# A graph network kernel: the third weight part of every second batch is multiplied on GpSimd

## What is computed

```python
def _spmm(src, dst, w, x, n):
    return jax.ops.segment_sum(w[:, None] * x[src], dst, num_segments=n)
...
msg = h[src] * norm[:, None]
out = jax.ops.segment_sum(msg, dst, num_segments=n_nodes)
```

## Time and profile before

| | us |
|---|---|
| median of the runs | 1826.44 |
| span of the profiled execution | 1822.0 |
| PE busy in it | 1704.3 (94%) |
| VectorE busy | 942.9 (52%) |
| ScalarE busy | 569.8 (31%) |
| GpSimd busy | 186.2 (10%) |
| mean granted TensorE clock | 0.989 of full |

### The profile page before, as it was taken

The page is one execution under the profiler, slowest core; times in us unless marked ns, Lnnn a source line. Parts: engine busy times, 40 slices in busy tenths (PEclk is TensorE's granted clock), DMA queues, the critical chain, the costliest instruction groups (busy, mean ns, idle before and its releaser), DMA issues.

```text
span 1822.0 us, 30852 instructions
## 1 busy us (share of the span) xinstructions
PE 1704.3 (94%) x10162; PEld 1363.7 (75%) x10163; DVE 942.9 (52%) x1593; ACT 569.8 (31%) x854; POOL 186.2 (10%) x260
## 2 busy tenths in 40 slices
PE   6999999888879999999999999999999999998995
PEld 4898988888766777777777777767677777787784
DVE  7999999998862300111144443552312243245436
ACT  2135677888880100000011111343400000004442
POOL 4000000000000100000000000000000000153683
PEclk9999999999999999999999999999999999999998
DMA  4203344544569445454443435900054434434375
GB/s 98 1 34 124 146 175 192 206 201 200 228 239 356 132 139 154 134 161 149 138 127 110 127 124 149 232 1 0 15 187 167 141 110 120 151 117 132 106 241 183
DMA packets 136919, 261.73 MB, mean 144 GB/s; under 512 B 22236, under 2 KB 74735, under 8 KB 136606
## 3 DMA queue, kind: packets, MB, share of 16 engines
q1 hardware_dynamic: 116824, 237.02, 40.2%
q0 software_dynamic: 5808, 14.70, 2.2%
q10 hardware_dynamic: 14230, 9.29, 1.7%
HBM read 161.13 MB, written 108.09 MB: 148 GB/s over the span
## 4 chain that ended last, share of the span: by engine, by line
issue 55%; PE 27%; ACT 6%; DVE 4%; ACTq 3%; DMA 2%; POOL 1%; DVEq 1%; SPq 0%; POOLq 0%
PE ps L2112 12%; PE ps L2113 4%; PE ps L2143 3%; ACT wide L870 3%; ACTq L914 2%; PE ps L2363 2%; ACT ps L818 2%; PE ps L2347 2%; DVE act_c L1373 1%; PE ps L2355 1%; PE ps L2339 1%; PE ps L2160 0%; ACTq L859 0%; DMA count_matrix<-wide 0%; PE ps L2015 0%
## 5 line engine op out<-in xcount | busy, mean ns | idle before, releaser
L2143 PE MATMUL ps<-wide 128*128 128x320 f32 (+1 forms) x2000 | 533.2, 427 | 0.0
L2143 PEld LDWEIGHTS ps<-wide 128*128 128x128 f32 x2000 | 378.4, 190 | 141.3 <-issue 0.4
L2112 PE MATMUL ps<-early,act_c 128*128 128x200 bf16 x2400 | 295.7, 252 | 43.4 <-issue 18.7
L2143 PE MATMUL ps<-wide,act_a 128*128 128x320 f32 (+1 forms) x1000 | 264.4, 426 | 2.3 <-DMA wide<-weight_matrix 2.2
L2112 PEld LDWEIGHTS ps<-early,act_c 128*128 128x128 bf16 x2400 | 220.5, 97 | 58.1 <-issue 57.3
L2143 PEld LDWEIGHTS ps<-wide,act_a 128*128 128x128 f32 x1000 | 189.8, 190 | 75.4 <-DMA wide<-weight_matrix 2.4
L870 ACT COPY wide<-ps 128x832 f32<-128x832 f32 x200 | 169.8, 849 | 121.8 <-PE ps L2113 120.6
L818 ACT ACTIVATE ps<-wide 128x832 f32 (+1 forms) x200 | 173.4, 868 | 42.0 <-ACT wide L870 33.7
L1373 DVE TENSOR_TENSOR act_c<-act_a,pair_tab 128x3072 bf16<-128x3072 bf16 x98 | 169.1, 1750 | 14.6 <-PE ps L2113 14.6
L1501 DVE TENSOR_TENSOR wide<-ps,rows 128x1280 f32<-128x1280 f32 x10 | 14.9, 1491 | 283.5 <-PE ps L2160 283.5
L2112 PE MATMUL ps<-act_a,act_c 128*128 128x200 bf16 x1152 | 140.3, 251 | 11.0 <-ACT ps L818 4.2
(11 more groups left out here) (261 smaller groups left out, 1808.5 us busy)
## 6 DMA issues: line engine op xcount, KB each, us to landing
wide<-weight_matrix SPq DMA_DIRECT2D x90, 800.0 KB, 4.5
wide<-count_matrix SPq DMA_DIRECT2D x45, 800.0 KB, 4.6
weight_matrix<-wide SPq DMA_DIRECT2D x60, 480.0 KB, 2.5
count_matrix<-wide SPq DMA_DIRECT2D x60, 480.0 KB, 2.6
weight_matrix<-wide SPq DMA_DIRECT2D x20, 560.0 KB, 2.7
count_matrix<-wide SPq DMA_DIRECT2D x20, 560.0 KB, 2.7
wide<-weight_matrix SPq DMA_DIRECT2D x20, 400.0 KB, 3.7
routed_tokens<-in_x_dram SPq DMA_DIRECT2D x2, 3072.0 KB, 30.4
```

The lines of the kernel that those rows point to most:

```text
L2112: nc.tensor.matmul(weights, hot_parts[:, slot % PART_SLOTS, part, two, :, k], hot_key[mask_slot][:, mask_two, 0:WCOLS, k], start=False, st ...
L2143: i = nc.tensor.matmul(ps[:, 2 * sub + h, 0:n], features[:, q * QUADS + t, h * P:(h + 1) * P], moving, start=q == 0 and t == 0, stop=q == ...
```

## The change

On every second batch (`slot % 2 == 1`) VectorE's product covers only the first two weight parts. The third is made by a new loop on GpSimd, one `tensor_tensor` per line of 128 x 1024 bf16 elements with both inputs in SBUF. It waits for `hot_lane` of its line and for the same point of `pair_done` as VectorE, and raises `thirds_made`, on which TensorE waits before the second batch of each line. On TensorE and ScalarE the register that a wait compares with passes through a bitwise "and" with 2047 first, which leaves its value as it is. Two semaphores of later weight loads are made one. What is added in the branch `disordered > 0` doesn't run with these inputs.

```diff
@@ TensorE, ScalarE: register waits
-                    act.wait_ge(pair_done, end)
+                    act.wait_ge(pair_done, act.scalar_reg_alu(ALU.bitwise_and, end, COUNTED))
...
-                            pe.wait_ge(acc_free, nc.s_assert_within(free, 1, WINDOWS // GROUP, skip_runtime_bounds_check_because="a group's number plus one"))
+                            pe.wait_ge(acc_free, pe.scalar_reg_alu(ALU.bitwise_and, free, COUNTED))
                             if half == 0:
                                 pe.wait_ge(batch_ready, step * UNROLL + batch + 1)
+                            if half == 0 and weighed_by_pool(batch):
+                                pe.wait_ge(thirds_made, step * MASK_SLOTS + batch // MASK_BATCHES + 1)
@@ GpSimd, after stage_end(pool, 1)
+            def third_parts(step, turns):
+                for half in range(turns):
+                    both_batches = step * MASK_SLOTS + half
+                    pool.wait_ge(lane_made, both_batches + 1)
+                    for b in range(MASK_BATCHES):
+                        slot = half * MASK_BATCHES + b
+                        if weighed_by_pool(slot):
+                            pool.wait_ge(pair_done, (both_batches + 2) * MASK_PAIRS + b * BATCH)
+                            third = slice(2, 3)
+                            pool.tensor_tensor(hot_parts[:, slot % PART_SLOTS, third], of_lanes(half, b, third), of_weights(step, slot, third), ALU.mult).then_inc(thirds_made, 1)
+
+            with pool.Fori(0, TURNS) as step:
+                third_parts(step, MASK_SLOTS)
+            third_parts(TURNS, TURNS_LEFT)
@@ VectorE
-                            pair_weights = pair_weight[:, ds(step * UNROLL + slot, 1), :, :].rearrange("p g j (a k) -> p (g j) a k", k=2)
-                            weighed = [P, 3, TWOS, P, 2]
+                            parts = slice(0, 2 if weighed_by_pool(slot) else 3)
                             dve.wait_ge(pair_done, (both_batches + 2) * MASK_PAIRS + b * BATCH)
-                            dve.tensor_tensor(hot_parts[:, slot % PART_SLOTS], hot_lane[half][:, b * TWOS:(b + 1) * TWOS].unsqueeze(1).broadcast_to(weighed),
-                                              pair_weights.unsqueeze(3).broadcast_to(weighed), ALU.mult).then_inc(batch_ready, 1)
+                            dve.tensor_tensor(hot_parts[:, slot % PART_SLOTS, parts], of_lanes(half, b, parts), of_weights(step, slot, parts), ALU.mult).then_inc(batch_ready, 1)
...
             compute_end(dve, 1)
+            dve.wait_ge(thirds_made, BATCHES // MASK_BATCHES)
@@ TensorE, in front of the last layer
-            pe.wait_ge(moe_w1_loaded, 16 * MOES)
-            pe.wait_ge(moe_w2_loaded, 16 * MOES)
+            pe.wait_ge(moe_weights_loaded, 16 * 2 * MOES)
```

More of the change, by code:

```diff
@@ L75 @@
 UNROLL = MASK_SLOTS * MASK_BATCHES
+COUNTED = 2047
 BATCHES = -(-STEPS_P // MASK_PAIRS) * MASK_BATCHES
@@ L467, in build_program @@
         lane_made = sem("lane_made")
+        thirds_made = sem("thirds_made")
         batch_ready = sem("batch_ready")
@@ L504, in build_program @@
         gcn_in = sem("gcn_in")
-        moe_w1_loaded = sem("moe_w1_loaded")
-        moe_w2_loaded = sem("moe_w2_loaded")
+        moe_weights_loaded = sem("moe_weights_loaded")
         biases_loaded = sem("biases_loaded")
@@ L574, in over_banks, with weighed_by_pool, of_weights, of_lanes @@
             return ps_flat[:, bank * 512:bank * 512 + PPAD]
+        def weighed_by_pool(slot):
+            return slot % MASK_BATCHES == 1
+        def of_weights(step, slot, parts):
+            weights = pair_weight[:, ds(step * UNROLL + slot, 1), parts, :].rearrange("p g j (a k) -> p (g j) a k", k=2)
+            return weights.unsqueeze(3).broadcast_to([P, parts.stop - parts.start, TWOS, P, 2])
+        def of_lanes(half, b, parts):
+            return hot_lane[half][:, b * TWOS:(b + 1) * TWOS].unsqueeze(1).broadcast_to([P, parts.stop - parts.start, TWOS, P, 2])
         def block_t_ps(bank, b):
@@ L722, in _ @@
                         here_e = slice(e * D, (e + 1) * D)
-                        sp.dma_start(moe_w1[:, :, here_e], a["L1_ffn_w1"][e].rearrange("(k p) n -> p k n", p=P)).then_inc(moe_w1_loaded, 16)
-                        sp.dma_start(moe_w2[:, :, here_e], a["L1_ffn_w2"][e].rearrange("(k p) n -> p k n", p=P)).then_inc(moe_w2_loaded, 16)
+                        sp.dma_start(moe_w1[:, :, here_e], a["L1_ffn_w1"][e].rearrange("(k p) n -> p k n", p=P)).then_inc(moe_weights_loaded, 16)
+                        sp.dma_start(moe_w2[:, :, here_e], a["L1_ffn_w2"][e].rearrange("(k p) n -> p k n", p=P)).then_inc(moe_weights_loaded, 16)
                     sp.dma_start(moe_b1, a["L1_ffn_b1"].rearrange("e n -> (e n)").partition_broadcast(P)).then_inc(biases_loaded, 16)
@@ L2092, in _ @@
                             pair(g, par)
+                pe.drain()
+                pe.sem_inc(pair_done, PPAD)
+                pe.sem_inc(lane_made, BATCHES // MASK_BATCHES)
             with pe.If(disordered < 1):
```

## The result

The changed kernel takes 1894.95 us, the median of four runs (1890.23 to 1901.01), against 1826.2 for the kernel before (four runs; the three of the first table had 1826.44). The ratio is 1.0385, with a 95% interval of 1.0364 to 1.0406. The prediction was 1914.5, within 1868 to 1990: slower, and by 20 us less than forecast. The profiled execution is the fastest of the four and has a span of 1888.5 us, 66.5 more than before.

The account below looks back on a forecast made before the run. VectorE was taken to bound the build's first half, with TensorE close behind. 74 lines x 7.83 = 579.4 us against 489.3 gave +90, corrected to +88: span 1910, plus 4.4 to the median, 1914.5, range 1868 to 1990.

Parts of the forecast that it names:

- What bounds the kernel: Matrix build: VectorE sets the pace in the first half at 6.34 us a line; ScalarE, TensorE and VectorE alternate later.
- TensorE's own pace: 5.90: Matrix build: TensorE needs 5.90 us a line, 16 pairs at 5.8 plus 0.1, the second limit 0.44 under VectorE.
- rival A: Matrix build: no exclusion, TensorE's 5.90 decides, 40 lines gain 0.44 us each, 18 us, to 1808; chance 0.09.
- Relief of 0.54 us: VectorE's line in the build: 1024 of 3072 elements fewer in one product takes 6.34 us to 5.80.
- Exclusion: Matrix build: GpSimd's product and VectorE's two-input stream exclude each other, so a line takes 5.80 + 2.03 = 7.83 us.
- Its size: Matrix build: a GpSimd product of 2.22 us, less handover, keeps VectorE away for 2.03 us per line.
- The two corrections: Late part and end of build: VectorE's 14.4 us of waits shrink to 3; ScalarE's 12.3 us tail to about 7, -5.
- Who wins doesn't matter: Matrix build: whichever engine gets the port first, each line holds VectorE's stream and GpSimd's 2 us.
- the second case: Matrix build: VectorE keeps GpSimd out, TensorE stops, VectorE runs out of free `hot_parts` buffers and pauses, giving GpSimd 2 us.
- The "ands" at 0: TensorE's sequencer in the build: four register operations per line, 296 in all, hidden while TensorE waits for VectorE; 0 us.
- The bound of 9.5 us: TensorE's sequencer in the build: cost of 296 "and" operations at 32 ns if all were exposed.
- The falling clock: Matrix build: exclusion plus TensorE idle 1.93 us a line lowers its clock; half the lines low gives about 2020; chance 0.07.

Follow-up runs that it names:

- relief with GpSimd silent: Changed kernel without GpSimd's product, "ands" kept; on every second batch nobody makes the third part and TensorE takes the second twice: 1841.66 us, ratio 1.0078.
- the product apart: Kernel with the "ands" alone, VectorE making all three parts, plus one GpSimd product per line between buffers of its own that nothing waits for: 1933.22 us, ratio 1.0576.
- the copy: Kernel with the "ands" alone, VectorE making all three parts, plus a GpSimd copy of 1024 bf16 elements per line between its own buffers: 1865.27 us.

## The prediction against the result

**What bounds the kernel: half right.** VectorE was busy without a gap, but it wasn't the only limit. "TensorE's own pace: 5.90" failed. It came from one stretch of 16 matmuls and one gap of 0.23 us, among the smallest; the others run to 1.4. Over whole stretches TensorE needs 6.42 to 6.57 us with the "ands" and 6.34 to 6.42 with half of them. It changed neither sign nor sum, since VectorE's 7.51 lies above, but it made rival A's 1808 wrong, at least with the "ands" in: relief with GpSimd silent gave 1841.7.

**Relief of 0.54 us: right.** The product of 2048 elements takes 1.21 us, and a line without the exclusion would be 7.51 - 1.70 = 5.81.

**Exclusion: right in kind.** VectorE's two-input stream and GpSimd's reads take turns, as rows 5 and 6 had it for other forms. The handshake is cleared by the product apart, which nobody waits for. The section "Who interferes with whom" in the Trainium skill's "SBUF — State Buffer" has the case as the runs show it, with the memset as its other half: a GpSimd instruction that only writes doesn't contend with a two-input VectorE instruction, and 951 ns of memset per line cost nothing. The prediction also took from this section that the lock is held for a whole instruction, and the section gives it to whoever issues first. There the measurement decides: VectorE lost 1.70 us where GpSimd's instruction is never shorter than 1.95, and a GpSimd instruction issued at 101.10 us stood behind every VectorE instruction of the next 96 us.

**Its size: the term that was mis-sized.** I took 2.03 us per line; it is 1.70. The row of 1.95 us for 896 elements gives GpSimd's duration, I scaled it to 2.22, and I took the hold on the port to be nearly all of it. Both steps were too high. VectorE loses the time of the reads alone, 2048 x 0.83 ns = 1.70. The median duration of 2.36 contains a wait for its turn of some 0.4 us, and the shortest, 1.95, is still 0.25 over the hold. 74 x 0.33 is 24 us of the sum's error. The two corrections came to -4.3 where I had -5, and to nothing where I had left 3; the 4.1 us after the build weren't in the sum. They and a median 6.5 us above the profiled span, where I had 4.4, took back 6 of the 27 us by which those terms were too high. So that the forecast is only 20 us off is in part luck.

**Who wins doesn't matter: right for the sum, and for a reason I had only half.** In the changed kernel GpSimd's product nearly always got in at the next boundary. Where nothing waited for it, it once stood 98 us, and the lines still came to 8.04 us on the mean. My reason for the second case, that TensorE stops and so forces VectorE to pause, wasn't put to the test: in the changed kernel no product took over 3.5 us.

**The "ands" at 0: right, as the run with twice as many shows.** The bound of 9.5 us for the exposed case was too low: a register operation shown with 32 ns costs TensorE 64 when its sequencer sets the pace.

**The falling clock: didn't happen.** TensorE's matmuls are idle 1.6 us in every line and its weight loads 1.8, less than the 2.08 us in front of the one fall of the earlier trace rows, and from 101 us on the granted clock stays at 1.00. With the product apart, where single waits reached 5.8 us, it did fall, and the stage was no longer for it.

## What to carry to other kernels

Work moved from a full VectorE to GpSimd isn't parallel when VectorE's instructions have two SBUF inputs: count what GpSimd reads, all inputs together, at the 0.83 ns per element and partition measured here for bf16, and add it to VectorE's time. Here 0.54 us went and 1.70 came. Before relieving an engine that is busy 100%, take away its work with nobody doing it and see what the kernel gains; here, with the "ands" in, it was nothing. And read the second engine's pace over a whole stretch, not over its best line.

## What was new about the hardware

- GpSimd's hold on the port is in proportion to the elements it reads: 1.70 us for 2 x 1024, 0.84 for 2 x 512, 0.84 for 1 x 1024, and none for 1024 written. It is 0.2 to 0.25 us shorter than the shortest durations of the same instructions.
- A GpSimd instruction can stand 98 us (136 and 116 in the runs with half the product and with the copy) in front of a VectorE stream without gaps, each of whose instructions is shorter than 2 us. In the changed kernel the longest of 74 took 3.5 us. All the long waits began in the first product of a line, but others that began there were short. What decides this wasn't found.
- The wait for the port is part of the waiting instruction's duration on VectorE, so its busy share rises from 52% to 54% with less work to do.
- A register operation shown with 32 ns in TensorE's sequencer costs 64 to 70 ns where the sequencer sets the pace, and nothing that shows where TensorE waits for VectorE.
